# Graph network kernel: radial network spread over the edge blocks, dense matmuls two groups later, TensorE waiting on the gather semaphores itself

## What is computed

```python
h = jnp.maximum(_layernorm(x), 0.0)
# L0: two graph convolutions ("layer 0" and "layer 1" of the kernel), each
#   h = layer_norm(h, g, be)
#   out = segment_sum(norm * (h @ W)[src], dst) + b + h @ lw.T + lb ; h = relu(out)
# x_final = relu0 + relu1 ; x = x + x_final @ pw.T + pb
h = jnp.maximum(_layernorm(x), 0.0)
# L1: node features through W_up0 / W_up1 (128 x 128); per edge a radial network
h = edge_feats                                  # 100000 x 8
for W in (W_mlp1, W_mlp2, W_mlp3):              # 8x64, 64x64, 64x64
    h = SILU_2MOM * jax.nn.silu(h @ W / jnp.sqrt(W.shape[0]))
tpw = h @ W_mlp4                                # 100000 x 512 weights
# messages = tpw times sender features times edge attributes, segment_sum over dst, W_out0 / W_out1
```

## Time and profile before

| what | value |
|---|---|
| median of 3 runs | 5891.26 us (5843.2 to 5891.44) |
| the profiled execution | 5896.5 us, its span 5894.7 us |
| engines busy over the span | PE 83%, DVE 48%, ACT 39%, POOL 46% |
| mean granted TensorE clock | 0.925 |
| first gather of layer 0 / layer 1 / tensor product | 535.5 / 1841.0 / 3433.4 us |

### The profile page before, as it was taken

The page is one execution under the profiler, slowest core; times in us unless marked ns, Lnnn a source line. Parts: engine busy times, 40 slices in busy tenths (PEclk is TensorE's granted clock), DMA queues, the critical chain, the costliest instruction groups (busy, mean ns, idle before and its releaser), DMA issues.

```text
span 5894.7 us, 104811 instructions
## 1 busy us (share of the span) xinstructions
PE 4878.7 (83%) x17136; PEld 2263.9 (38%) x17137; DVE 2857.1 (48%) x8231; ACT 2308.6 (39%) x6178; POOL 2737.7 (46%) x3492
## 2 busy tenths in 40 slices
PE   6897566778886567787777889999999999999988
PEld 5443122333332123333333334444444444444444
DVE  7542122334442112222222257777777777777776
ACT  0441000111110012233333466666666666666665
POOL 0334766666664766654433234444443333333332
PEclk9998678889997678899899999999999999999999
DMA  2233666677775666776666534444444334333333
GB/s 81 96 107 125 185 187 205 210 219 232 230 233 153 183 201 207 227 234 200 198 186 182 176 115 120 117 116 116 119 118 119 115 115 118 115 116 115 117 115 97
DMA packets 433673, 916.80 MB, mean 156 GB/s; under 512 B 63094, under 2 KB 170870, under 8 KB 433511
## 3 DMA queue, kind: packets, MB, share of 16 engines
q0 software_dynamic: 195840, 641.89, 37.5%
q1 hardware_dynamic: 237798, 274.56, 14.2%
HBM read 787.79 MB, written 128.41 MB: 155 GB/s over the span
## 4 chain that ended last, share of the span: by engine, by line
PE 31%; issue 21%; DVE 10%; DMA 8%; ACT 8%; DVEq 7%; ACTq 5%; POOL 5%; POOLq 2%; another core or an unknown queue 2%; SPq 1%
PE bank L1220 7%; DMA ring<-tab_d,idx 6%; POOL ring L559 4%; PE bank L1269 3%; PE bank L1350 3%; PE bank L1191 3%; PE bank L1193 3%; DVEq L1078 3%; ACT hB L756 3%; ACT dense_w L767 3%; ACTq L753 2%; PE bank L1253 2%; DVE hA L1086 2%; DMA tw<-tab_d 2%
## 5 line engine op out<-in xcount | busy, mean ns | idle before, releaser
L559 POOL DMA_INDIRECT ring<-tab_d,idx x1568 | 1541.6, 983 | 909.4 <-issue 549.1
L1350 PE MATMUL bank<-dense_w,oh 128*128 128x512 f32 x3520 | 1619.8, 603 | 66.9 <-DVE dense_w L1095 66.4
L1220 PE MATMUL bank<-ring,ohp 128*128 x3904 | 1084.6, 439 | 422.2 <-POOLq L569 330.9
L525 POOL DMA_INDIRECT ring<-up_d,idx x880 | 880.4, 1000 | 498.4 <-POOL idx L521 348.6
L767 ACT ACTIVATE dense_w<-hA,hC 128x128 f32<-128x128 f32 x2640 | 820.2, 389 | 654.8 <-DVE hA L1086 600.1
L1350 PEld LDWEIGHTS bank<-dense_w,oh 128*128 128x128 f32 x3520 | 633.1, 190 | 858.8 <-issue 668.1
L1220 PEld LDWEIGHTS bank<-ring,ohp 128*128 x3904 | 421.1, 108 | 1065.7 <-issue 763.6
L983 DVE TENSOR_TENSOR ohp<-iota_w,dst_f 128x512 f32 x392 | 266.1, 691 | 703.5 <-PE bank L1220 513.6
L521 POOL COPY idx<-src_i 128x2 int32 x440 | 81.2, 185 | 1045.2 <-DVE dense_w L1095 964.2
L1340 PE MATMUL bank<-w,hC 64*128 64x256 f32 x3520 | 501.9, 403 | 31.4 <-issue 22.9
L1072 DVE SCALAR_TENSOR_TENSOR hA<-ring,hC,hB 128x128 f32<-128x128 f32 x880 | 270.4, 348 | 490.3 <-ACT hB L756 428.3
(11 more groups left out here) (180 smaller groups left out, 4877.2 us busy)
## 6 DMA issues: line engine op xcount, KB each, us to landing
hC<-hid_d SPq DMA_DIRECT2D x440, 64.0 KB
tab_d<-tout SPq DMA_DIRECT2D x98, 256.0 KB, 2.7
tw<-tab_d SPq DMA_DIRECT2D x98, 256.0 KB
hlw<-hl_d SPq DMA_DIRECT2D x98, 256.0 KB
ring<-tab_d,idx POOLq DMA_INDIRECT x1568
hid_d<-hC SPq DMA_DIRECT2D x98, 256.0 KB
hl_d<-agg SPq DMA_DIRECT2D x74, 256.0 KB, 3.0
ring<-up_d,idx POOLq DMA_INDIRECT x880
```

Source lines behind the costliest of these rows:

```text
L525: g_.indirect_dma_start(ring_v[:, b, k, :], None, table, bass.IndirectOffsetOnAxis(idx_t[:, b, k:k + 1], 0)).then_inc(S["got"][b], 16)
L559: g_.indirect_dma_start(ring_h[:, b, k, :], None, table, bass.IndirectOffsetOnAxis(idx_b[:, b, k:k + 1], 0)).then_inc(S["got"][b], 16)
L1220: ins = pe.matmul(bank[0][:, :], ohp_b[:, bass.ds(at, 1), k, :].rearrange("p b n -> p (b n)"), ring_b[:, bass.ds(slot, 1), k, h, :].rearra ...
L1350: ins = pe.matmul(bank[h][:, :], oh[:, b, k, :], msg[:, b, k, h, :], start=False, stop=False, skip_group_check=True)
```

## The change

1. GpSimd no longer raises `arrived`. Before the third row of a block it waits for the gathers of five blocks ago, whose `idx` slot it is about to overwrite.
2. TensorE waits on the ring slot's own semaphore `got[b]`, chosen by `pick`, a tree of branches over the six slots.
3. The window's own rows `tw` are added at the end of the sum and no longer at its start, and end it, in place of the zero matmul `touch`.
4. In layer 0, `turn` stands before `edge_sum` and takes the window of two steps back, `dense` the same window after `edge_sum`; `high`, `low` and the stores come one step later. In layer 1, `turn_xs` and `turn_h` stand before `edge_sum` and `project` and `up` behind it, on windows two and four steps back. `up` writes `bank[7]`.
5. The radial network runs inside layer 1's edge loop: in block n, TensorE does `layer3(n)`, `layer2(n+1)`, `layer1(n+2)` after the visit, and ScalarE the three activations, for the first 94 blocks; the first groups come before the loop, the last ones after it. Each layer has one bank, one `hA` and one `hB`, where there were two each. ScalarE issues `load_ef` and `store_hid`, each behind a wait for its predecessor's landing.

```diff
             g_.wait_ge(S["idx_ready"], copied)
             g_.reg_add(d, d, 1)
             row(0)
             row(1)
-            with g_.If(n > LAG):
-                g_.wait_ge(S["got"][(b - LAG) % NK], landed)
-                g_.nop().then_inc(S["arrived"], 1)
+            with g_.If(n > NK - 1):
+                g_.wait_ge(S["got"][(b + 1) % NK], landed)
             g_.tensor_copy(idx_b[:, (b + 1) % NK, :], src_i[:, bass.ds(ahead, BT)]).then_inc(S["idx_ready"], 1)
             row(2)
             row(3)
...
 # TensorE, edge_sum
     after(pe, S["y_read"], w)
-    pe.wait_ge(S["self_in"], (w + 1) * 16)
-    pe.matmul(bank[0][:, :], ident_h[:, :], tw[:, 0:D], start=True, stop=False, skip_group_check=True)
-    pe.matmul(bank[0][:, :], ident_h[:, :], tw[:, D:], start=False, stop=False,
-              skip_group_check=True).then_inc(S["self_used"], 1)
...
         visit(slot, at, True)
+    else:
+        touch(bank[0][:, :], D, True)
     with pe.Fori(lo, hi) as g:
         v, n = pe.snap(v_r), pe.snap(c)
         slot, at = pe.snap(n % NK), pe.snap(v % NV)
-        pe.wait_ge(S["arrived"], n)
+        landed = pe.snap((n + (NK - 1)) // NK * (16 * BT))
+        pick(pe, pe.snap(n % NK), 0, NK, lambda b: pe.wait_ge(S["got"][b], landed))
         pe.wait_ge(S["onehot"], v)
-        visit(slot, at)
+        visit(slot, at, False)
+        if L == 1:
+            with pe.If(n < NG // 4 - 3):
+                layer3(n)
+                layer2(n + 1)
+                layer1(n + 2)
         pe.reg_add(c, c, 1)
-    touch(bank[0][:, :], D, False).then_inc(S["sum_done"], 1)
+    pe.wait_ge(S["self_in"], (w + 1) * 16)
+    pe.matmul(bank[0][:, :], ident_h[:, :], tw[:, 0:D], start=False, stop=False, skip_group_check=True)
+    pe.matmul(bank[0][:, :], ident_h[:, :], tw[:, D:], start=False, stop=True,
+              skip_group_check=True).then_inc(S["sum_done"], 1)
...
 # TensorE's lists
-    peeled(pe, [(0, edge_sum), (1, turn), (1, dense)])
+    peeled(pe, [(2, turn), (0, edge_sum), (2, dense), (3, lambda w: None)])
-    peeled(pe, [(2, layer2), (0, edge_sum), (1, turn_xs), (3, layer3), (2, turn_h), (1, project), (2, up),
-                (0, layer1), (4, lambda w: None)])
+    peeled(pe, [(2, turn_xs), (4, turn_h), (0, edge_sum), (2, project), (4, up)])
...
 # SP's lists
-    peeled(sp, [(0, load_self), (0, load_hl), (1, store_r), (2, store_tab), (2, store_hl)])
+    peeled(sp, [(0, load_self), (0, load_hl), (1, store_r), (3, store_tab), (3, store_hl)])
-    peeled(sp, [(0, load_ef), (0, load_self), (3, store_up), (0, load_hl), (4, store_hid), (0, load_r0),
-                (1, load_x), (2, store_x1)])
+    peeled(sp, [(0, load_self), (0, load_hl), (0, load_r0), (2, load_x), (3, store_x1), (4, store_up)])
...
 # ScalarE
+    def load_ef(i):
+        if not isinstance(i, int) or i > 1:
+            ac.wait_ge(ef_in, i * 16)
+            ac.wait_ge(m1, i - 1)
+        to = ...
+        ac.dma_start(to, a["ef_t"][:, bass.ds(i * D, D)]).then_inc(ef_in, 16)
+    def store_hid(i):
+        ac.wait_ge(a3, i + 1)
+        if not isinstance(i, int) or i > 0:
+            ac.wait_ge(hid_out, i * 16)
+        ...
+    def radial(w, c=c):
+        lo, hi = block_range(ac, w)
+        with ac.Fori(lo, hi) as g:
+            n = ac.snap(c)
+            with ac.If(n < NG // 4 - 3):
+                act3(n)
+                act2(n + 1)
+                act1(n + 2)
+                store_hid(n)
+                load_ef(n + 3)
+            ac.reg_add(c, c, 1)
-    peeled(ac, [(1, relu_r), (2, high), (1, std), (1, scaled), (1, copy_at)])
+    peeled(ac, [(1, relu_r), (3, high), (2, copy_at), (1, std), (1, scaled)])
-    peeled(ac, [(1, act1), (1, relu_r), (2, std), (2, relu_h), (2, act2), (1, copy_xT), (3, act3),
-                (2, copy_hT), (2, up_out), (4, lambda w: None)])
+    peeled(ac, [(1, relu_r), (2, copy_xT), (4, copy_hT), (0, radial), (3, std), (3, relu_h), (4, up_out)])
...
 # VectorE's lists
-    peeled(ve, [(1, layer_out), (0, onehots), (2, low), (1, second_norm)])
+    peeled(ve, [(1, layer_out), (0, onehots), (3, low), (1, second_norm)])
-    peeled(ve, [(1, layer_out), (0, onehots), (1, project_in), (2, residual)])
+    peeled(ve, [(1, layer_out), (0, onehots), (1, project_in), (3, residual)])
```

More of the change, by code:

```diff
@@ L723, in act3, with act1 @@
-                def act3(j):
-                    for b in range(2):
-                        after(ac, hid_out[b], j, 16)
-                        ac.wait_ge(m3, j * 2 + 1 + b)
-                        ac.activation(hC[:, b, :], bank[4 + b][:, :], ACT.Silu).then_inc(a3, 1)
+                    ac.copy(uo[:, :], bank[7][:, :]).then_inc(S["up_ready"], 1)
+                def act1(i):
+                    ac.wait_ge(m1, i + 1)
+                    if not isinstance(i, int) or i > 0:
+                        ac.wait_ge(m2, i)
+                    ac.activation(hA[:, 0, :], bank[4][:, :], ACT.Silu).then_inc(a1, 1)
@@ new lines, in act2, with act3 @@
+                def act2(i):
+                    ac.wait_ge(m2, i + 1)
+                    if not isinstance(i, int) or i > 0:
+                        ac.wait_ge(m3, i)
+                    ac.activation(hB[:, 0, :], bank[5][:, :], ACT.Silu).then_inc(a2, 1)
+                def act3(i):
+                    ac.wait_ge(m3, i + 1)
+                    to = hC[:, i % 2, :] if isinstance(i, int) else hC[:, bass.ds(i % 2, 1), :].rearrange("p b n -> p (b n)")
+                    ac.activation(to, bank[6][:, :], ACT.Silu).then_inc(a3, 1)
@@ L1222, in visit @@
                                                 ring_b[:, bass.ds(slot, 1), k, h, :].rearrange("p b n -> p (b n)"),
-                                                start=False, stop=False, skip_group_check=True)
+                                                start=(first and k == 0 and h == 0), stop=False, skip_group_check=True)
                         ins.then_inc(S["used"], 1)
@@ L1274, in turn_h @@
                     pe.wait_ge(S["h_ready"], w + 1)
-                    after(pe, S["up_ready"], w)
+                    after(pe, S["hT_ready"], w)
                     for i in range(4):
@@ L1321, in _ @@
+                    layer3(0)
+                    layer2(1)
+                    layer1(2)
+                    peeled(pe, [(2, turn_xs), (4, turn_h), (0, edge_sum), (2, project), (4, up)])
+                    last = NG // 4 - 1
+                    layer3(last - 2)
+                    layer2(last - 1)
+                    layer1(last)
+                    layer3(last - 1)
+                    layer2(last)
+                    layer3(last)
                     pe.wait_ge(a3, NG // 4)
```

123 lines of the change are left out of this document (59 added, 64 removed).

## The result

The changed kernel took **5700.53 us** (median of 4 runs, 5691.99 to 5706.0) against 5891.35 for the kernel before beside it: ratio 0.9692, 95% interval 0.9639 to 0.9744. The forecast was 5394. Its profiled span is 5690.0 us at a mean clock of 0.940; 204.7 of the 5894.7 us are gone where 498 had been forecast.

The account below looks back on a forecast made before the run. No engine is full in layers 0 and 1; GpSimd's landing waits bind mostly, TensorE's order in late layer 1. 98 + 26 + 289 + 43 + 8 + 38 - 4 = 498 off 5896.5 gives 5398.5, median 5394 us; range 5290 to 5570.

Parts of the forecast that it names:

- Gathers without the relay ... 98 saved: Early layer 0, first 30 windows: waiting for five blocks ago removes the landing wait, 863 us for 961.
- I take ... 5.3 a block: GpSimd's gather loop: price of a block without the relay, chosen between 5.13 and 5.70 us.
- The gathers keep their pace: First rival, chance 0.15: more transfers in flight each take longer, a block stays at 5.9 us; 5564 us in all.
- Late layer 0 ... 26 saved: Last 19 windows of layer 0: turn and copy hidden by visits, TensorE and GpSimd compete; 266 us for 292.
- Late layer 1 ... 289 saved: Last 37 windows of layer 1: xT and `tw` waits and radial network go; 607 us for 896, 30 allowed for DMA.
- Radial network in the loop ... 43 saved: Layer 1's first 12 windows: radial work fits in TensorE's idle at 4.33 us a block; 573 us for 616.
- its landing waits ask for transfers issued a block earlier: ScalarE in layer 1's radial blocks: 2.9 us a block, working a block ahead of TensorE's need.
- The branches on TensorE ... I take 0: Six-way `pick` on TensorE: bounds 0 and 0.5 us a block, taken as 0; at 0.5 the time is 5440.
- Ends: GpSimd's idle after each layer's last window, 49.2 and 79.7 us, falls to 43 and 42: 8 and 38 saved.
- The tensor product's 2462 us included, stays: Tensor product after layer 1: unchanged, apart from 4 us lost to late radial groups delaying its first loads.
- TensorE binds in the radial blocks: Rival, chance 0.13: layer 1's first windows keep clock 0.76, a block costs 5.7 us, 670 for 573; 5491 in all.
- Slower: Rival, chance 0.03: TensorE's tree, register waits and If must pass 2.5 us a block; at 3 us some 6085.

Follow-up runs that it names:

- set E: Follow-up runs on a fifth, fast chip, where the kernel before took 5788 us and the unchanged changed kernel 5459.41 us, ratio 0.9428.
- half_bytes: Changed kernel with each gathered row 1 KB in place of 2 KB in layers 0 and 1; 5698.4 us, a single run.
- half_gathers: Changed kernel with two of each block's four gathers left out; 5156.77 us, ratio 0.8919.
- relay_back2: Changed kernel with GpSimd's wait and relay put back and no tree on TensorE, run again on another chip; 5715.37 us, ratio 0.9873.
- hybrid: Layer 0 as in the changed kernel; layer 1 with the relay restored and load_ef at the top of ScalarE's block; 5491.63 us, ratio 0.9486.
- ef_early: Changed kernel with load_ef(n+3) moved from the end of ScalarE's block to its top; 5649.29 us, ratio 0.9602.
- tree_back: Changed kernel with the relay put back and the six-way `pick` tree added behind the relay's wait; 5745.05 us, ratio 0.9925.
- ef_relay: Changed kernel with the relay put back, no tree on TensorE, and load_ef at the top of ScalarE's block; 5674.63 us, ratio 0.9563.
- mixed: Changed kernel with the relay only in layer 1's radial-network blocks and load_ef at the top of ScalarE's block; 5400.16 us, ratio 0.9326.
- tree_only: Kernel before with its relay kept and the six-way `pick` tree added on TensorE behind the relay's wait; 6028.6 us, ratio 1.0155.
- two_trees: Changed kernel with TensorE passing its six-way branch and wait twice for each block; 5635.19 us, ratio 0.9742.
- relay_back: Changed kernel with GpSimd's wait for the block before and its relay put back, no tree on TensorE; 5728.84 us, ratio 0.9743.
- relay_only: Kernel before with only the relay removed: GpSimd waits for five blocks ago, TensorE on slot semaphores through the tree; 6078.22 us, ratio 1.0339.
- shallow_only: Kernel before with TensorE on slot semaphores through the tree, GpSimd's wait for the block before kept without its relaying instruction; 5864.93 us, ratio 1.0140.
- set C: Follow-up runs on one slow chip, where the kernel before took 5932.83 us and the unchanged changed kernel 5756.94 us, ratio 0.9703.
- sets B, D, E: Follow-up runs on three different fast chips, where the kernel before took 5785, 5790 and 5788 us.
- sets A and C: Follow-up runs on two different slow chips, where the kernel before took 5881 and 5938 us.
- after_third: Changed kernel unchanged, on a fifth chip, against the kernel before; 5459.41 us, ratio 0.9428.

## Why the prediction was right and wrong

The sign and the largest term were right, the size was 306 us off. Of that, 131 us are the radial network in the loop, 70 early layer 0, 44 late layer 1, and the rest the ends and the tensor product. By steps:

- **"Gathers without the relay ... 98 saved": 28.** The landing wait goes as put, and the 5.09 to 5.13 us of the earlier trace rows is the right price of a block for GpSimd while its own instructions run at their usual speed: set E's chip has 834 us, below the 863 forecast. On the chip of the measurement the step that failed is "I take ... 5.3 a block": it holds nothing for slower instructions on GpSimd, and 168 register and branch instructions came to 118 us there, part of them hidden; 938 us was measured, 103 more than on set E's chip. This was the first rival, "The gathers keep their pace", in its number and not in its reason, that each transfer takes longer with more in flight: half_bytes moves half the bytes at the same pace, and the time stands between the gathers. The argument against the rival took 5.70 us from one block of window 0; the mean of that window before is 5.88 (170.4 us for 29 blocks), and with the wait kept it is 5.87 to 5.95 on fast chips and slow ones alike, so no row of the kernel before could tell them apart.
- **"Late layer 0 ... 26 saved": 25,** and 52 on set E's chip. On the first chip this is in part luck: half_gathers puts TensorE's own time at 242, my 259 had its terms too high, and gathers slower than costed made that up (268; in that stretch TensorE still stands 14.3 us before visits, on set E 1.1).
- **"Late layer 1 ... 289 saved": 245,** and 328 with set E's pace (against the same first profile of before). The three removed parts went as costed: in those windows TensorE waits once for `tw`, 1.2 us, and never for xT. The 30 us of allowance for the DMA engines were too little on one kind of chip and not needed on the other (share 0.85 for 568 us).
- **"Radial network in the loop ... 43 saved": 88 lost.** This is the step that failed most, on two terms that the sum put at nothing. First, "its landing waits ask for transfers issued a block earlier" is true of ScalarE's waits, but TensorE's `layer1` also waits for the edge features, and their load is issued at the end of ScalarE's block: by the records TensorE could use it from 1909.64, it was issued at 1907.11 and had landed at 1910.52. The sum has no term for that wait. It costs 37 us on one chip (relay_back2 to hybrid, whose layer 0 differs) and 26 to 39 by ef_early. Second, **"The branches on TensorE ... I take 0"**: 28 us here by tree_back. Table loads are small beside them (13 us, within what chips differ by). With both mended ef_relay has 635 us, hybrid 621 and mixed 630, for 573 forecast and 618 to 625 before. What keeps these there is at least in part the relay's pace: in hybrid GpSimd waits 68 times, 55.0 us, for landings. No run has deep gathers without a tree, so the size of the rest is **open**; with half the gathers, and both faults in it, the stretch took 632.
- **"The branches on TensorE"** cost more than in that stretch. The row that decided it, 24 matmuls without a gap, shows a loop and register arithmetic but no tree, and stands behind dense work, which likely gave the sequencer a lead: in tree_only late layer 0 loses nothing and late layer 1 loses 94 us. The other row was GpSimd's 0.50 us, and a compare-and-branch takes 0.04 us on GpSimd and 0.17 on TensorE (the medians above). The trace of the kernel before had TensorE's price in the branch that ends its block loop, which the prediction didn't read: 41 of them from 1498 to 1790 us, median 0.21 us (L1232). My upper bound of 0.5 us was too low: some 0.9 us of sequencer time, of which 0.46 a block reach the end (two_trees), 0.96 where TensorE is the bound (tree_only, late layer 1). The Trainium skill, Advanced Engine Details and Errata (Control Flow Timing), gave an estimated 0.4 to 0.5 us by its 108 ns for a compare-and-branch and 51 ns for a plain one; this case disagrees, with 65 to 218 ns for a compare-and-branch on TensorE and about twice the estimate for a tree.
- **Ends: -5 and 22 for 8 and 38.** GpSimd runs up to six blocks ahead, so when it is through, TensorE has more left (relay_back: 40 and 43 us, my 43 and 42): the gain moved into the stage ahead.
- **"The tensor product's 2462 us included, stays": 24 longer.** The last radial groups end later: from the first copy to the first matmul 14.2 us in place of 6.2, so 8 (ef_early has 11.3). The other 15 us are spread over all of its gathers and aren't explained; every kernel with the new order has them (2475.8 to 2488.9 us in all, against 2462.3 to 2464.8).
- **"TensorE binds in the radial blocks" by the clock** fell: it was granted 0.90 there. TensorE does bind there, by the load and the branches: on set E GpSimd waits 189.0 us for its visits. "Slower" had the right engine and place, but set 2.5 us a block as the price at which the gain is gone, against the 0.9 measured. It came true when the relay's part was tried alone: relay_only +197 us. Of this tree_only explains 94 of 102 us in late layer 1. The 44 us in its first windows, where tree_only loses 5 and shallow_only some 3, need the depth of the gathers too: there GpSimd has 114 register and branch instructions of over 0.5 us, 79 us in all, and the kernel before has none. That they cause the 44 us is likely and not shown.

So the size depends on the chip too: with the same code the change is worth 3.1% in the first measurement, 3.0% in set C and 5.7% in set E. Even there it is under the 8.5% forecast.

## What to carry to other kernels

A wait that is taken away shows what stood behind it, and that can be a thing that no trace of the kernel before shows and that differs from chip to chip: forecast the old pace as a case of its own beside the shorter one. Price a chain of branches by the rows of the engine that passes it, per block, less what its sequencer's lead hides, and leave the relay to an engine that is waiting in any case: the best version here relays in the blocks with the radial network and waits directly elsewhere. When a load moves into another engine's loop, write down for every engine that waits for it when it is issued and when it is needed, and measure on more than one chip where gathers in flight set the pace.

## What the runs showed of the hardware that I had not expected

- The pace of the same indirect gathers (four of 128 rows of 2 KB a block) differs by chip when they run freely: 5.26 to 5.38 us a block in window 0 on three chips (sets B, D, E), 5.87 to 6.06 in the first measurement and in sets A and C. On the slower ones GpSimd's branches and register arithmetic between gathers, 0.04 to 0.14 us as a rule, now and then take 0.7 us each. When each block waits for the one before, the five chips where that ran (all but set E's) need 5.87 to 5.95, and the slow instructions all but disappear.
- Half the bytes per row didn't change the slower pace (941 us for 938, DMA share 0.41 for 0.69).
- A compare-and-branch took a median of 0.17 us on TensorE's sequencer and 0.04 on GpSimd's (after_third). A six-way tree of them takes TensorE's sequencer about 0.9 us, and a second one as much again.
